# First cross-attention: probabilities transposed in ten packed blocks, V in block form placed by small loads, a third fold on Pool, weights rounded by ScalarE

## The chip, the cores and the metric

The kernel runs on one core of one Trainium2 chip. The metric is the device time of one execution in microseconds (us). TensorE is called PE here, VectorE DVE, ScalarE ACT, GpSimd Pool, and the queue that issues the loads and stores SP. The time before is 2041.48 us, the median of three runs (2040.95, 2041.48 and 2046.44).

## What is computed

Two gated layers on `x` of 4 batches x 1024 tokens x 256, with a context of 4 x 77 x 256. Only the first step of the first layer is touched:

```python
x = x + tanh(g_xattn[0]) * L0_xattn(layernorm(x), ctx, ctx, wq, bq, wk, bk, wv, bv, wo, bo)

# L0_xattn: DIM = 256, 16 heads of 16, SCALE = 16 ** -0.5
qh = heads(q @ wq.T + bq);  kh = heads(k @ wk.T + bk);  vh = heads(v @ wv.T + bv)
attn = softmax(einsum('bhqd,bhkd->bhqk', qh * SCALE, kh))
out = einsum('bhqk,bhkd->bhqd', attn, vh)          # 77 keys
return merge_heads(out) @ wo.T + bo
```

After it come a feed-forward net with ternary weights (1024 hidden), a second cross-attention of 8 heads, and a gated self-attention.

## The kernel before, in words

`gated_layers` runs four stages one after the other: `first_attention` (tag A), `feed_forward` (F), `cross_attention` (C) and a self-attention (E). The change is in `first_attention` alone, which takes the first 255 us or so of the span.

In that stage the 4096 tokens are 16 pairs `n` of 256 tokens, each pair two tiles `T` of 128 (so 32 tiles), four pairs to a batch. `STEPS` runs from -12 to 34, and every engine goes through the same steps in an order written out by hand. In step `T`, with `n, odd = divmod(T, 2)`:

- PE: `scores(T + 2)`; the first two groups of `p_transpose(T)`; `reciprocals(n - 1)` in an odd step or `x_transpose(n + 2)` in an even one; the other two groups of `p_transpose(T)`; `q_proj(n + 2)` (odd); `pv(n - 1, odd)`; `out_proj(n - 2)` (even); and once per batch, in odd steps, `k_proj` and `v_proj`.
- ACT: `prob_out(T, g)` empties PSUM behind the transposes, with `r_evacuate` or `x_evacuate` between the second and third group; then `q_evacuate` (odd), `exp(T + 2)`, `k_evacuate` once per batch, and `layer_norm(n + 3)` (even).
- DVE: `weigh(n - 2)` (even), `row_max(T + 2)`, `shift(T + 2)`, `recip_sum(T + 1)`, `ln_stats`, `v_evacuate` once per batch, `residual(n - 2)` (even), and `mantissas(i)` in the steps of `CHUNK_STEPS`.
- Pool: a third of the Newton step of the next batch's root (`root`), `fold(T + 2)`, `widen(T)`, `add_bias(n)` (odd), and `round_chunk(i)` in the steps of `CHUNK_STEPS`.
- SP: loads and stores in one in-order queue. The chunks are the 22 pieces (128x1024 f32) of the next stage's weights, which are staged in `w_stage` and rounded to fp32r on the way. Chunk `i` is loaded when chunk `i - STAGE` has been rounded (`p_rounded`) and looked at by DVE (`d_bits`).

`p_transpose(T, g)` transposes four heads: per head a 128x77 piece of `prob` is the stationary operand and the identity the moving one, and a 77x128 piece of PSUM comes out. There are two PSUM buffers `ps_t` for the groups, so that group `u` waits for the evacuation of group `u - 2` (`t_out`). A tile has 16 such transposes and four evacuations of 77x512. `pv(n, part)` multiplies the transposed probabilities by V: eight products of 32 columns each, in two rounds over the four column groups of the array; each product is two MATMUL records in the trace. V stands in `vcol`, with 16 of 32 columns filled per head. `fold` halves the 78 columns of `prob` twice on Pool (39, then 20 of 40 padded), and `recip_sum` adds the 20 that are left on DVE.

`scores` has one PSUM buffer: `scores(T + 1)` waits for `shift(T)` (`d_sub`). `layer_norm(n)` waits on ACT for the root of its whole batch (`root_done`); for the first batch DVE works it out in `ln_stats(3)`. `x_transpose(1)` waits for `v_made`, since V's projection of batch 0 stands at step -2 and shares the PSUM buffer `ps_m`.

## Time and profile before

| what | value |
|---|---|
| median of three runs | 2041.48 us |
| the profiled execution | 2043.89 us, its span 2042.2 us |
| PE busy over the span | 1862.7 us (91%) |
| DVE, ACT, Pool busy | 1203.0, 1102.7, 701.8 us |
| stage A, 0 to 256 us | PE 215.11, DVE 189.79, ACT 154.34, Pool 154.35 us busy |

The page gives the busy time of an engine as the sum of its instructions' spans. Matmuls are pipelined: the mean duration of a transpose is 288 ns while the next one starts after about 120 ns, so that what a group of matmuls costs is read from the start of the group to the start of the next group in the timeline, not from a mean duration. Stage F begins when the last pair of stage A has been stored.

### The profile page before, as it was taken

The page shows a single profiled execution, that of the slowest core. Times are in us where ns is not written, and L with a number is a line of the kernel's source. Part 1 is how long each engine was busy: PE and PEld are TensorE (multiplying, and loading weights), DVE is VectorE, ACT ScalarE, POOL GpSimd, SP SyncE. Part 2 cuts the span into 40 slices and gives each one's busy share as a digit, 9 for nine tenths or more (in the row PEclk, how much of TensorE's full clock was granted, in tenths as well). Part 3 has the DMA queues.
Part 4 walks back from the last instruction along what each step waited for, and adds up shares of the span by engine and source line. Part 5 has one row for each costly group of instructions (what it writes and reads, how often), then busy time and mean ns, then how long its engine had stood idle before and what let it go on. Part 6 is the DMA issues. An engine that isn't in the chain of part 4 may idle for free. (4 is left out here: it accounts for less than half of the span.)

```text
span 2042.2 us, 62044 instructions
## 1 busy us (share of the span) xinstructions
PE 1862.7 (91%) x27265; PEld 1520.6 (74%) x27265; DVE 1203.0 (59%) x1687; ACT 1102.7 (54%) x1920; POOL 701.8 (34%) x893
## 2 busy tenths in 40 slices
PE   4999859999999999996799986899999999999986
PEld 3677648888887878875688865778888877887865
DVE  7787532433324333232455535888888888888882
ACT  4677433444434434342455433777777667777761
POOL 3777400100000000100333322556556565655541
PEclk9999979999999999998899997999999999999997
DMA  5222000000000000001101004322332242223110
GB/s 172 81 78 67 27 26 1 21 21 1 21 1 21 21 0 21 0 21 54 64 27 34 23 22 139 87 60 60 101 96 60 60 116 81 65 70 112 55 45 24
DMA packets 135942, 104.95 MB, mean 51 GB/s; under 512 B 9379, under 2 KB 132104, under 8 KB 135688
## 3 DMA queue, kind: packets, MB, share of 16 engines
q1 hardware_dynamic: 135688, 101.19, 16.6%
q8 instruction: 205, 3.36, 0.7%
q14 instruction: 49, 0.40, 0.1%
HBM read 76.00 MB, written 25.17 MB: 50 GB/s over the span
## 5 line engine op out<-in xcount | busy, mean ns | idle before, releaser
L2122 ACT ACTIVATE E_prob<-E_ps_s,E_negmax 128x1024 f32<-128x1024 f32 x256 | 284.7, 1114 | 144.2 <-DVE E_negmax L2436 143.8
L2436 DVE TENSOR_REDUCE E_negmax<-E_ps_s 128x1 f32<-128x1024 f32 x256 | 301.5, 1219 | 88.5 <-PE E_ps_s L1941 88.1
L2443 DVE STREAM_TRANSPOSE E_prob<-E_prob 128x1024 f32<-128x1024 f32 x256 | 304.0, 1226 | 24.0 <-ACT E_prob L2122 11.7
L1960 PEld LDWEIGHTS E_ps_o<-E_prob,E_vrep 32*64 32x64 f32 x15872 | 231.8, 130 | 65.9 <-ACT E_part L2148 56.2
L1960 PE MATMUL E_ps_o<-E_prob,E_vrep 32*64 32x128 f32 x15872 | 263.5, 274 | 13.8 <-issue 4.4
L1544 ACT ACTIVATE F_raw<-F_ps,ffn_scales 128x512 f32<-128x512 f32 x128 | 88.1, 688 | 288.2 <-PE F_ps L1454 288.2
L1454 PE MATMUL F_ps<-F_ha,ffn_w_rounded 128*128 128x512 f32 x1024 | 240.5, 396 | 0.0
L1454 PE MATMUL F_ps<-F_hb,ffn_w_rounded 128*128 128x512 f32 x1024 | 240.2, 395 | 0.0
L1454 PEld LDWEIGHTS F_ps<-F_hb,ffn_w_rounded 128*128 128x128 f32 x1024 | 192.5, 188 | 46.5
L1454 PEld LDWEIGHTS F_ps<-F_ha,ffn_w_rounded 128*128 128x128 f32 x1024 | 191.4, 188 | 47.8 <-issue 1.6
L2338 POOL TENSOR_TENSOR E_part<-E_part 128x512 f32<-128x512 f32 x93 | 119.3, 1283 | 253.8 <-ACT E_part L2148 253.8
L1631 DVE TENSOR_TENSOR F_ha<-F_raw,F_ha 128x512 fp32r<-128x512 f32 x64 | 44.3, 693 | 184.2 <-ACT F_ha L1546 184.2
L1631 DVE TENSOR_TENSOR F_hb<-F_raw,F_hb 128x512 fp32r<-128x512 f32 x64 | 44.4, 693 | 169.1 <-ACT F_hb L1546 169.1
L1454 PE MATMUL F_ps<-F_xt_part,ffn_w_rounded 128*128 128x512 f32 x512 | 125.1, 402 | 11.2 <-DVE F_raw L1621 6.3
L89 POOL TENSOR_TENSOR F_rs<-F_rs 128x4 f32<-128x4 f32 x27 | 5.4, 198 | 358.9 <-DVE F_rs L1592 357.5
L1941 PE MATMUL E_ps_s<-E_k_hi,E_q_hi 64*128 64x512 f32 x512 | 114.7, 443 | 14.1 <-ACT E_prob L2122 12.7
L1454 PEld LDWEIGHTS F_ps<-F_xt_part,ffn_w_rounded 128*128 128x128 f32 x512 | 95.2, 191 | 38.8 <-DVE F_raw L1621 10.6
L1564 POOL TENSOR_TENSOR F_xt_part<-F_xt,F_xt_part 128x1024 fp32r<-128x1024 f32 x9 | 21.6, 2401 | 294.1 <-DMA x<-A_x 149.9
L1941 PE MATMUL E_ps_s<-E_k_hi,E_q_lo 64*128 64x512 f32 x512 | 102.3, 394 | 0.0
L1941 PE MATMUL E_ps_s<-E_k_lo,E_q_hi 64*128 64x512 f32 x512 | 101.2, 390 | 0.0
L472 ACT ACTIVATE A_pt<-A_ps_t 77x512 f32<-77x512 f32 x128 | 69.3, 591 | 28.2 <-PE A_ps_t L359 28.0
L1621 DVE SCALAR_TENSOR_TENSOR F_raw<-F_ps,ffn_scales,F_silu 128x512 f32<-128x512 f32 x64 | 47.5, 750 | 61.8 <-ACT F_silu L1528 61.6
(284 smaller groups left out, 3937.6 us busy)
## 6 DMA issues: line engine op xcount, KB each, us to landing
E_vrep<-E_v_all SPq DMA_DIRECT2D x128, 256.0 KB, 3.1
A_w_stage<-in_L_ffn_h_wT SPq DMA_DIRECT2D x16, 512.0 KB, 4.1
E_v_all<-E_vst SPq DMA_DIRECT2D x32, 256.0 KB, 2.2
F_x<-x SPq DMA_DIRECT2D x9, 512.0 KB, 3.8
A_x<-in_x SPq DMA_DIRECT2D x16, 256.0 KB, 5.6
x<-A_x SPq DMA_DIRECT2D x16, 256.0 KB, 2.2
x<-F_x SPq DMA_DIRECT2D x8, 512.0 KB, 2.9
C_x<-x SPq DMA_DIRECT2D x16, 256.0 KB, 5.5
```

Source lines behind the costliest of these rows:

```text
L472: act.activation(pt[:, n % 2, 4 * g:4 * g + 4, t * TOK:(t + 1) * TOK], ps_t[0:S, g % 2, :].rearrange("s (h q) -> s h q", h=4), ACT.Copy).t ...
L1454: mm = pe.matmul(out, fw.chunk(w, name, k, j * P, (j + 1) * P), a[:, k, :], start=k == 0 and i == 0, stop=k == K - 1 and i == len(parts) - 1)
L1544: act.activation(raw[:, u % 2, :], ps[:, u % 4, :], ACT.Gelu, scale=scale).then_inc(u_raw, 1)
L1564: pool.tensor_tensor(xt_part[1][:, :, :], xt[:, :, :], xt_part[0][:, :, :], ALU.subtract).then_inc(xt_lo, 1)
L1621: dve.scalar_tensor_tensor(out=dst, in0=ps[:, 2 * (j % 2) + 1, :], scalar=scales[:, 1, j:j + 1], in1=silu[:, j % 2, :], op0=ALU.mult, op1= ...
L1631: dve.tensor_tensor(dst, raw[:, u % 2, :], hi, ALU.subtract).then_inc(u_lo, 1)
L1941: mm = pe.matmul(ps_s[:, j, keys], a[rows, c % 2, cols], k[rows, c % 2, keys], start=i == 0, stop=i == 2)
L1960: mm = pe.matmul(low[64 * j:64 * j + 64, g, :], vrep[rows, slot, KB // 4 * (quarter % 2) + k, dh * j:dh * (j + 1)], prob[rows, u % 2, :, j ...
L2122: act.activation(prob[:, s // UT % 2, s % UT, j, :], ps_s[:, j, :], ACT.Exp, bias=negmax[:, at:at + 1], scale=1.0, accum_out=den[:, 2 * c ...
L2338: pool.tensor_tensor(part[:, 0, :], part[:, 0, :], part[:, 1, :], ALU.add).then_inc(part_added, 1)
L2436: dve.tensor_reduce(negmax[:, at:at + 1], ps_s[:, j, :], AX.X, ALU.max, negate=True).then_inc(d_max, 1)
L2443: dve.transpose(at, at).then_inc(d_t, 1)
```

## The change

- `p_transpose` no longer goes head by head. `prob` becomes 1280 columns (`prob_all`: 16 heads of 78 packed, and 32 columns of zeros), and ten blocks of 128 columns are transposed, in groups of 4, 4 and 2. The first group stands ahead of `reciprocals` or `x_transpose`, the other two behind. `prob_out` empties 128x512, 128x512 and 128x256.
- V is laid out for these blocks (`v_blk`, 17 tiles of 128x32): a head's rows stand where the packed probabilities have them. DVE writes V once to `v_sb`, and SP copies it into place by `place_v(b)`, 25 loads per batch of 5 to 77 rows of 64 bytes, since a head's 77 rows can lie across a border of two blocks. `pv` has nine products in part 0 and eight in part 1; the ninth is a third round on one column group.
- Pool folds a third time (20 to 10 columns), and `recip_sum` adds 10.
- `round_chunk` goes from Pool to the end of ACT's step, with `STAGE` 4 in place of 3.
- The first pair gets a root of its own (`root_pair`, from the first two tiles' statistics), and the batch's whole root is then worked out again by DVE for the other pairs.
- V's projection of batch 0 moves from step -2 to -1, and `x_transpose(1)` waits for `q_made` alone.
- The loads of `x` 1 to 3 go behind `wq`. The memsets of `prob_all` and `v_blk` stand on DVE behind the biases, ahead of the first statistics. `place_v(0)` stands in SP's queue behind chunk 4 and ahead of `x` 8 to 11 and chunk 5; `place_v(b + 1)` stands at pair `4 b + 1`.

```diff
-STAGE = 3
+STAGE = 4
...
+    KC = -(-H * S2 // P)
+    GROUPS = [range(k, min(k + 4, KC)) for k in range(0, KC, 4)]
+    NG = len(GROUPS)
+    SEG = HR * S2
+    parts_of = {(g, c): range((g * C + c) * SEG // P, ((g * C + c + 1) * SEG - 1) // P + 1)
+                for g in range(RG) for c in range(C)}
...
         def v_step(b):
 
-            return 2 * PB * b - 3 if b else -2
+            return 2 * PB * b - 3 if b else -1
...
+            def place_v(b):
+
+                sp.wait_ge(v_made, b + 1)
+                if b >= 2:
+                    sp.wait_ge(e_pv, PB * (b - 1))
+                for g, c, j, k, row, n, s0 in v_pieces():
+                    at = (HC * c + HR * g + j) * dh
+                    sp.dma_start(v_blk[row:row + n, b % 2, tile_of[g, c, k], dh * j:dh * (j + 1)],
+                                 v_sb[s0:s0 + n, at:at + dh]).then_inc(s_vblk[b % 2], 16)
...
             load_chunk(STAGE)
+            sp.wait_ge(s_pad, 1)
+            place_v(0)
             for n in range(2 * PB, XR):
                 load_x(n)
...
+                if n % PB == 1 and n // PB + 1 < B:
+                    place_v(n // PB + 1)
                 while at < CHUNKS and CHUNK_STEPS[at - STAGE] <= 2 * n + 2:
                     load_chunk(at)
...
-                elif n % PB == 1:
+                elif n == 2 or n % PB == 1 and n > 1:
                     pe.wait_ge(v_made, n // PB + 1)
...
-                for j in range(4):
-                    mm = pe.transpose(ps_t[0:S, g % 2, j * TOK:(j + 1) * TOK], prob[:, T % PR, 4 * g + j, 0:S],
+                for i, k in enumerate(GROUPS[g]):
+                    mm = pe.transpose(ps_t[:, u % 2, i * TOK:(i + 1) * TOK], prob_all[:, T % PR, k * P:(k + 1) * P],
                                       ident[:, :])
...
-                        h = HC * part + HR * g + j
-                        mm = pe.matmul(ps_o[RT * g:RT * (g + 1), part, :], vcol[:, b % 2, h, :],
-                                       pt[:, n % 2, place(h), :], start=j == 0, stop=j == HR - 1)
+                        ks = parts_of[g, part]
+                        if i < len(ks):
+                            mm = pe.matmul(ps_o[RT * g:RT * (g + 1), part, :], v_blk[:, b % 2, tile_of[g, part, ks[i]], :],
+                                           pt[:, n % 2, ks[i], :], start=i == 0, stop=i == len(ks) - 1)
...
                 if 0 <= T < TILES:
-                    for g in range(G // 2):
-                        p_transpose(T, g)
+                    p_transpose(T, 0)
...
+            def round_chunk(i):
+                act.wait_ge(s_chunk[i % STAGE], 16 * (i // STAGE + 1))
+                act.activation(ffn.w[:, i * WCH:(i + 1) * WCH], w_stage[:, i % STAGE, :], ACT.Copy).then_inc(a_rounded, 1)
...
                 if not odd and 0 <= n + 3 < NP:
                     layer_norm(n + 3)
+                if T in CHUNK_AT:
+                    round_chunk(CHUNK_AT[T])
...
+                own.step(pool.tensor_tensor(quarter[:, :, :], half_sum[:, :, 0:HALF // 2],
+                                            half_sum[:, :, HALF // 2:HALF], ALU.add))
...
+                pool.tensor_tensor(eighth[:, T % 2, :, :], quarter[:, :, 0:HALF // 4],
+                                   quarter[:, :, HALF // 4:HALF // 2], ALU.add).then_inc(p_eighth, 1)
...
+                if n == 0:
+                    own.wait()
+                    for t in range(2):
+                        own.link(dve.bn_aggr(mv0[:, t, :], stats[:, t, :]))
+                    own.wait()
+                    whole_root(mv0, rs0).then_inc(root_pair, 1)
...
-                for j in range(HR):
-                    ins = dve.tensor_tensor(dst[:, :, j, j * dh:(j + 1) * dh], src[:, :, j, :], vb[:, :, j, :], ALU.add)
-                ins.then_inc(v_made, 1)
+                dve.tensor_tensor(v_sb[:, :], ps_m[0:S, 0:HD], vbias[:, :], ALU.add).then_inc(v_made, 1)
...
-            dve.memset(prob[:, :, :, S:S2], 0.0)
-            dve.memset(half_sum[:, :, S2 // 2:HALF], 0.0).then_inc(s_pad, 1)
-            own.link(dve.memset(vcol[:, :, :, :], 0.0))
+            dve.memset(half_sum[:, :, S2 // 2:HALF], 0.0)
...
+            dve.memset(prob_all[:, :, :], 0.0)
+            dve.memset(v_blk[:, :, :, :], 0.0).then_inc(s_pad, 1)
```

`whole_root` is the guess, three Newton steps and the last two products, which before stood in `ln_stats` for the first batch only.

## Rows read from the trace of the kernel before

**Rows 1.** Busy time by engine from step 1 to step 29; start:end, length, engines, clock.
```profile
core 0: us, PE busy (x) PEld busy (x) DVE busy (x) ACT busy (x) POOL busy (x), PEclk, DMA share, GB/s
41.31:231.09 189.78, 177.54 (x1685) 133.06 (x1685) 151.36 (x205) 131.49 (x233) 134.04 (x185) 0.98 0.22 65
```

**Rows 2.** PE's timeline, steps 26 (even) and 27 (odd): start, length, line.
```profile
209.01 0.81 PE L348 MATMUL A_ps_s<-A_kt,A_q 32*128 32x154 f32 x16
209.75 1.10 PE L359 MATMUL A_ps_t<-ident,A_prob 128*77 128x128 f32 x8
210.68 0.60 PE L304 MATMUL A_ps_m<-ident,A_xn 128*128 128x128 f32 x4
211.19 1.11 PE L359 MATMUL A_ps_t<-ident,A_prob 128*77 128x128 f32 x8
212.23 1.07 PE L375 MATMUL A_ps_o<-A_pt,A_vcol 77*32 77x256 f32 x16
213.23 1.99 PE L392 MATMUL A_ps_m<-A_wo,A_o 128*128 128x256 f32 x8
215.15 0.81 PE L348 MATMUL A_ps_s<-A_kt,A_q 32*128 32x154 f32 x16
215.89 1.10 PE L359 MATMUL A_ps_t<-ident,A_prob 128*77 128x128 f32 x8
216.83 0.60 PE L331 MATMUL A_ps_m<-ident,A_r_wide 128*128 128x128 f32 x4
217.33 1.12 PE L359 MATMUL A_ps_t<-ident,A_prob 128*77 128x128 f32 x8
218.29 1.97 PE L316 MATMUL A_ps_m<-A_xt,A_wq 128*128 128x256 f32 x8
...
221.19 0.81 PE L348 MATMUL A_ps_s<-A_kt,A_q 32*128 32x154 f32 x16
```

**Rows 3.** Groups by line and form, 0 to 268 us: busy, mean ns, idle before.
```profile
L472 ACT ACTIVATE A_pt<-A_ps_t 77x512 f32<-77x512 f32 x128 | 69.3, 591 | 28.2 <-PE A_ps_t L359 28.0
L530 POOL TENSOR_TENSOR A_half_sum<-A_prob 128x624 f32<-128x624 f32 x32 | 49.5, 1546 | 71.9 <-ACT A_prob L477 65.4 <-DVE A_rsum L642 3.3 <-issue 2.3
L477 ACT ACTIVATE A_prob<-A_prob 128x1232 f32<-128x1232 f32 x32 | 39.4, 1232 | 13.9 <-DVE A_prob L634 13.9
L534 POOL TENSOR_TENSOR A_quarter<-A_half_sum 128x320 f32<-128x320 f32 x32 | 30.6, 957 | 2.5
L554 POOL CAST ffn_w_rounded<-A_w_stage 128x1024 fp32r<-128x1024 f32 x22 | 23.2, 1056 | 0.3 <-DMA A_w_stage<-in_L_ffn_w_wT 0.3
```

**Rows 4.** ACT's timeline around the start of step 26.
```profile
208.84 1.23 ACT L477 ACTIVATE A_prob<-A_prob 128x1232 f32<-128x1232 f32 x1
210.45 1.08 ACT L472 ACTIVATE A_pt<-A_ps_t 77x512 f32<-77x512 f32 x2 [0.37 <-PE A_ps_t L359]
```

**Rows 5.** Timelines of the start: DVE's memset, ACT's first LayerNorm, DVE's third maximum.
```profile
1.18 0.91 DVE L688 MEMSET A_vcol<- 77x1024 f32 x1
14.34 1.09 ACT L435 ACTIVATE A_xn<-A_x,A_rs 128x256 f32<-128x256 f32 x2 [3.19 <-DVE A_rs L612]
38.27 1.43 DVE L619 TENSOR_REDUCE A_negmax<-A_ps_s 128x16 f32<-128x1232 f32 x1
```

**Rows 6.** Timeline of PE: steps 1 and 3, and the wait of step 11.
```profile
41.31 1.41 PE L348 MATMUL A_ps_s<-A_kt,A_q 32*128 32x154 f32 x16 [5.43 <-DVE A_prob L634]
58.46 1.96 PE L359 MATMUL A_ps_t<-ident,A_prob 128*77 128x128 f32 x8 [3.31 <-ACT A_pt L472]
112.80 1.11 PE L359 MATMUL A_ps_t<-ident,A_prob 128*77 128x128 f32 x8 [1.38 <-ACT A_pt L472]
```

**Rows 7.** SP's queue at the start: issue of a small load, of x, of chunks.
```profile
2.83 0.47 SPq L233 DMA_DIRECT2D A_qbias<-in_L_xattn_bq  x1
16.37 2.13 SPq L206 DMA_DIRECT2D A_x<-in_x  x4
19.67 13.35 SPq L216 DMA_DIRECT2D A_w_stage<-in_L_ffn_h_wT  x3
```

**Rows 8.** DMA issues by line: KB each, median us from issue to landing.
```profile
E_vrep<-E_v_all SPq DMA_DIRECT2D x128, 256.0 KB, 3.1
A_w_stage<-in_L_ffn_h_wT SPq DMA_DIRECT2D x16, 512.0 KB, 4.1
A_x<-in_x SPq DMA_DIRECT2D x16, 256.0 KB, 5.6
```

More of the change, by code:

```diff
@@ L186, in first_attention @@
         x_taken, q_made, k_made, v_made = (sem(n) for n in ("x_taken", "q_made", "k_made", "v_made"))
-        d_sub, a_exp, p_quarter, d_r, p_wide = (sem(n) for n in ("sub", "exp", "quarter_summed", "r", "r_widened"))
+        d_sub, a_exp, p_eighth, d_r, p_wide = (sem(n) for n in ("sub", "exp", "eighth_summed", "r", "r_widened"))
         r_taken = sem("r_taken")
@@ L233, in _ @@
                 sp.dma_start(dst, src).then_inc(s_small, 16)
-            load_x(2)
-            load_x(3)
             load_w(2, wq, wqT)
+            for n in range(1, PB):
+                load_x(n)
             for i, g in enumerate(gates_src):
@@ L410, in _ @@
                 if 0 <= T < TILES:
-                    for g in range(G // 2, G):
+                    for g in range(1, NG):
                         p_transpose(T, g)
@@ L420, in _ @@
                     k_proj((T + 5) // 8)
-                if (T + 3) % 8 == 0 and 1 <= (T + 3) // 8 < B:
-                    v_proj((T + 3) // 8)
+                for b in range(B):
+                    if T == v_step(b):
+                        v_proj(b)
         @block.scalar
@@ L492, in _ @@
                 if 0 <= T < TILES:
-                    for g in range(G // 2):
-                        prob_out(T, g)
+                    prob_out(T, 0)
                 if odd and 0 <= n - 1 < NP:
@@ L499, in _ @@
                 if 0 <= T < TILES:
-                    for g in range(G // 2, G):
+                    for g in range(1, NG):
                         prob_out(T, g)
```

121 lines of the change are left out of this document (67 added, 54 removed).

## The prediction

> **What bounds the kernel now.** I read the table of stretches first, then the timelines of PE, ACT, DVE and SP for stage A, then the groups by line. From step 1 to step 29 PE is busy 177.5 of 189.8 us, DVE 151.4, ACT 131.5, Pool 134.0 [rows 1]. So PE is the bound of the stage once it has started, with a fifth of the time spare on DVE and three tenths on the others. The timeline of steps 26 and 27 shows what this means: each group starts where the last one ends, with no gap [rows 2]. From scores to scores an even step takes 215.15 - 209.01 = 6.14 us and an odd one 221.19 - 215.15 = 6.04, a pair 12.18. Fourteen pairs would be 170.5 us, the projections of K and V some 6; the other 13 us of the 189.8 are waits and stretches of low clock. I look for two things: what leaves PE's pair, and which waits of the other engines come up when the pair is shorter. Ahead of step 1 PE isn't the bound: at 41.31 it had waited 5.43 us for DVE's shift [rows 6].
>
> **PE's pair.** Eight transposes take 0.93 and 1.04 us in the even step and 0.94 and 0.96 in the odd one, 3.87 for the 32 of a pair, 0.12 each [rows 2]. The new ones have 128 columns of weights and not 77. The nearest row is the transposes of x and of the reciprocals, which are 128x128: four take 0.51 and 0.50 us, 0.126 each [rows 2]. Twenty make 2.5 and a tail of 0.1, so 1.27 us leave the pair. V's product gets a third round in part 0. Two rounds take 1.00 us now, and one whole-width product takes 1.92 / 4 = 0.48 (out_proj) [rows 2]. The lone product needs its column group to itself behind two rounds, so I take 0.48; by mere issue (16 records in 1.00 us, two more) it would be 0.12. The net is -0.79 us per pair (bounds -1.4 and, if a transpose cost by its width, +0.5). The first pair lies in the start, so 14.5 pairs: **-11.5 us**.
>
> The Trainium skill ("TensorE: Matmul & The Clock Gate", LDWEIGHTS) speaks against this: a weight load costs by its columns, so that ten loads of 128 columns would cost what sixteen of 77 do. By that rule the transposes gain nothing. The full-width rows above disagree as to the pace, and I weigh it as a rival.
>
> **ACT.** Per tile 4 evacuations at a pitch of 0.49 (two in 1.08 us less the overlap) [rows 4] become two and one of 256 columns. From 1232 columns in 1.23 and 512 in 0.59 us [rows 3] the last is about 0.36, so ACT gains 0.6 us per tile, 19 us in all. The 22 roundings come to it: 1024 columns by the same line, 1.03 us, 23 us. Busy time stays about as it is, and ACT isn't the bound by it. The place matters: in an odd step the rounding stands behind exp(T + 2). Exp ran from 208.84 to 210.07 [rows 4], 1.06 us into step 26, and the first evacuation followed at 210.45. With a rounding between, it starts at S + 2.0 and is done at S + 2.6 (S is the start of the step's scores). PE wants that buffer back for its third group after 0.74 of scores, 4 transposes, 0.5 of x and 4 transposes: S + 2.25. What is queued behind that wait on PE is the last two blocks, V's products and out_proj, so the 0.4 us go onto the path. Fourteen chunks stand in odd steps: 11 at 0.4 and three at 0.8, where k_evacuate stands there too: 6.8, of which the first two are in the start. **+6 us** (bounds 0 and 10). In the three even steps with a chunk ACT has time.
>
> **Pool and DVE.** Pool loses 22 x 1.06 = 23 us and gets 32 folds of 160 columns. From 624 in 1.55 and 320 in 0.96 [rows 3] one is about 0.6 with its wait, 19 us. Its fold chain is 0.6 longer, and done before recip_sum asks for it within 0.5 us. Nothing is due of it until residual, which waits for out_proj anyway: zero, and up to 0.5 per odd step if DVE is late. The cast ahead of the last third of a batch's root leaves, a fold comes: the root is 0.45 us sooner. At step 11 PE waited 1.38 us behind ACT's wait for it [rows 6], and at two other places: **-0.9 us**. DVE gets 0.17 us less per tile. In steps 4 to 7 and 12 to 15, where statistics, chunks, V and the guess meet, DVE's work comes to 25 to 27 us against PE's new 23.5 for four steps (sums of its timeline there); it can lag 1.5 us before scores wait. **+1.5 us** (0 to 5).
>
> **The start.** The memsets now clear 3840 + 1088 columns ahead of the statistics, at 0.91 us per 1024 [rows 5] 4.4 us; three pairs' statistics leave the first root's way, about 2. The first LayerNorm, at 14.34 before [rows 5], comes at about 15.6, and the second, behind a second root of 3.7 us, at 22, 5 us later. The rest is given back in part by x_transpose(1), which no longer waits for V. DVE's third maximum, at 38.27 [rows 5], comes at 40 to 41, and V of batch 0 is made at about 39.
>
> Then SP issues 25 loads. A small load holds the queue 0.47 us [rows 7], so this is 11.8 us (10 to 13). Behind stand x 8 to 11 (2.13 us [rows 7]) and chunk 5: issued at about 53, landed 4.1 to 5.6 us later [rows 8], at 57 to 59. Before, the queue had issued chunks 4 to 6 by 33 [rows 7]. ACT wants chunk 5 at the end of step 1, at about 51, and waits 6.5 us; behind it stands the evacuation of step 2's first group, and so PE's transposes. DVE's mantissas(5) wait for the same load, behind them two passes of 1.43 us [rows 5] until scores(5). That puts q_proj of step 3 at about 65. Before, step 3 lost 3.31 us to the root and went on at 58.46, at the low clock [rows 6], with q_proj at 60.2: this old wait is covered by the new one. **+4.5 us** (1 to 9). V itself lands in time: 51 + 3.1 [rows 8] is where pv(0) falls. The later placements have four steps or more until a chunk behind them is due.
>
> The Trainium skill ("DMA: Bandwidth & Descriptors", Anatomy of one DMA) holds that the fixed cost of a load is nearly all completion latency, setup being small. Alone, it would let the 25 overlap in some 2 us, and the start would cost 1 and not 4.5. The issue rows contradict it for this queue.
>
> **Sum.** -11.5 + 6 - 0.9 + 1.5 + 4.5 = -0.4 us on the profiled 2043.9, so 2043.5. The profiled execution is 2.4 us over the median, which gives 2041.1: **2041 us**.
>
> **Rivals.**
> 1. PE's gain goes through. For it: ACT's busy time doesn't grow, and the two roundings of the start may slip into idle time. If the rounding is hidden (0 for 6) and the start costs 1 to 2, the sum is -11.5 - 0.9 + 1.5 + 1.5 = -9.4: 2032. Against it: ACT's place behind exp leaves no gap in rows 4. Chance 0.30.
> 2. ACT stands before chunk loads. If an issue takes 0.53 us, as in the four loads of x, and the chunk 6.5 us to land behind 1 MB of x, chunk 5 is there at 63 and the start costs 9; the same queue delays the chunks behind place_v(2) and place_v(3), and each rounding then costs its 0.6. -11.5 + 9 + 9 + 3 - 0.9 = +8.6: 2050. It decides from the point where chunk 5 lands 10 us after ACT asks for it. For it: SP's queue is in order; against it: small SBUF loads may issue faster than 0.47. Chance 0.18.
> 3. Transposes cost by the width of the weights (the rule above): 0.12 x 128 / 77 = 0.2 each, no gain, and V's third round: +0.48 per pair. 14.5 x 0.48 + 6 - 0.9 + 1.5 + 4.5 = +18: 2059. The 0.126 of rows 2 speaks against it. Chance 0.04.
>
> The forecast itself has 0.48. The range, 2031 to 2051, takes in most of rivals 1 and 2. 0.3%, about what a measurement of this kernel tells from no change, is 6 us: faster 0.30, same 0.48, slower 0.22.
>
> **What would show it.** In a pair of the late stretch without chunks: scores to scores 11.3 to 11.4 us; groups of four transposes at 0.50 and the last two at 0.25; V's part 0 at 1.45 and part 1 at 1.0. In even steps behind an odd chunk: PE idle 0.4 us before the last group, released by ACT. On SP: 25 issues in 10 to 13 us from about 39. ACT idle some 6 us before the first rounding of the loop, released by a DMA. Clock near 1.00 but for some us at 60. I am wrong on the fast side if the loads issue in under 0.3 us or the roundings leave no wait, on the slow side if DVE or a chunk's load holds PE in every batch.

## The result and the profile after

The changed kernel takes 2052.56 us, the median of 13 runs (2046.88 to 2056.19), where the kernel before took 2041.15 us beside it (13 runs). The ratio is 1.0051, 95% interval 1.0039 to 1.0063: slower by half a per cent, and clear of the spread. The prediction was 2041 us, no change, with a range to 2051; the time lies 1.6 us above that range, and "slower" had a chance of 0.22. The profiled execution of the changed kernel took 2047.0 us, 5.6 under its median; from the last matmul of stage C to the end, which the change doesn't touch, it took 805.4 us, where the profiled executions of all the other kernels took 807.7 to 817.6 (the kernel before 813.9), so I read the stages one by one and not the two spans against each other.

The page of the changed kernel, busy time by engine and the instruction queue (packets, MB, share):

```profile
PE 1847.7 (90%) x27105; PEld 1499.5 (73%) x27105; DVE 1199.1 (59%) x1703; ACT 1101.2 (54%) x1910; POOL 695.2 (34%) x903
...
q8 instruction: 221, 3.62, 0.7%
```

PE is busy 15 us less and the kernel is slower all the same. Three places tell why. First the steady stretch, PE's timeline of steps 26 and 27, which answers to [rows 2]:

```profile
205.92 0.81 PE L384 MATMUL A_ps_s<-A_kt,A_q 32*128 32x154 f32 x16
206.66 0.66 PE L395 MATMUL A_ps_t<-ident,A_prob 128*128 128x128 f32 x4
207.15 0.60 PE L340 MATMUL A_ps_m<-ident,A_xn 128*128 128x128 f32 x4
207.59 0.60 PE L395 MATMUL A_ps_t<-ident,A_prob 128*128 128x128 f32 x4
208.56 0.41 PE L395 MATMUL A_ps_t<-ident,A_prob 128*128 128x128 f32 x2 [0.38 <-ACT A_pt L513]
208.90 1.50 PE L413 MATMUL A_ps_o<-A_pt,A_v_blk 128*32 128x256 f32 x18
210.32 1.99 PE L430 MATMUL A_ps_m<-A_wo,A_o 128*128 128x256 f32 x8
212.25 0.81 PE L384 MATMUL A_ps_s<-A_kt,A_q 32*128 32x154 f32 x16
212.99 0.66 PE L395 MATMUL A_ps_t<-ident,A_prob 128*128 128x128 f32 x4
213.48 0.60 PE L367 MATMUL A_ps_m<-ident,A_r_wide 128*128 128x128 f32 x4
213.91 0.92 PE L395 MATMUL A_ps_t<-ident,A_prob 128*128 128x128 f32 x6
214.91 1.97 PE L352 MATMUL A_ps_m<-A_xt,A_wq 128*128 128x256 f32 x8
216.80 1.07 PE L413 MATMUL A_ps_o<-A_pt,A_v_blk 128*32 128x256 f32 x16
217.81 0.41 PE L384 MATMUL A_ps_s<-A_kt,A_q 32*128 32x154 f32 x4
```

From the start of four packed transposes to the start of the next group is 0.49 us, V's part 0 takes 210.32 - 208.90 = 1.42 and part 1 1.01. The odd step is 217.81 - 212.25 = 5.56 (6.04 before), the even one 6.33 (6.14 before), because it pays 0.38 us of ACT's wait ahead of the last two blocks. ACT's timeline of the same moment, beside [rows 4], has the reason, the rounding between exp and the first evacuation:

```profile
205.75 1.23 ACT L519 ACTIVATE A_prob<-A_prob 128x1232 f32<-128x1232 f32 x1
206.87 1.06 ACT L529 ACTIVATE ffn_w_rounded<-A_w_stage 128x1024 fp32r<-128x1024 f32 x1
207.82 0.59 ACT L513 ACTIVATE A_pt<-A_ps_t 128x512 f32<-128x512 f32 x1
```

Over steps 4 to 29 the table of stretches gives 162.10 us for the changed kernel (77.20 to 239.30); in the kernel before the same steps ran from 64.8 to 231.1, 166.3 us. The stretch is 4.2 us shorter.

```profile
77.20:239.30 162.10, 149.19 (x1405) 104.24 (x1404) 131.85 (x185) 113.39 (x198) 116.88 (x171) 1.00 0.23 71
```

Second, the start: timelines of SP, ACT and PE, beside [rows 7] and [rows 6].

```profile
37.98 19.57 SPq L257 DMA_DIRECT2D A_v_blk<-A_v  x25
57.60 2.04 SPq L229 DMA_DIRECT2D A_x<-in_x  x4
59.74 7.03 SPq L239 DMA_DIRECT2D A_w_stage<-in_L_ffn_h_wT  x5
...
65.15 1.06 ACT L529 ACTIVATE ffn_w_rounded<-A_w_stage 128x1024 fp32r<-128x1024 f32 x1 [16.27 <-DMA A_w_stage<-in_L_ffn_h_wT]
...
66.83 0.66 PE L395 MATMUL A_ps_t<-ident,A_prob 128*128 128x128 f32 x2 [16.75 <-ACT A_pt L513]
67.42 2.78 PE L413 MATMUL A_ps_o<-A_pt,A_v_blk 128*32 128x256 f32 x18
```

The 25 placement loads hold SP for 19.6 us, chunk 5 is issued at 59.7, ACT waits 16.3 us for it and PE 16.8 us for ACT. PE then works on at the slower pace: V's 18 records take 2.78 us instead of 1.50, at a granted clock of 0.50 from 67.42 to 70.20. Step 4's scores come at 77.2, before at 64.8: 12.4 us later. Stage A is left 8.7 us later (first transposes of stage F at 280.48, before at 271.81).

Third, stage F, in which nothing was edited. From its first transposes to the end of its last `F_ps` product, some 9 us before its last matmul, it lasts 679.0 us, before 673.7. All lengths of stage F below are taken so. PE's timeline at two starts of a tile, and the kernel before at the place of the first:

```profile
626.96 3.99 PE L1503 MATMUL F_ps<-F_xt_part,ffn_w_rounded 128*128 128x512 f32 x16 [1.65 <-issue]
797.78 5.54 PE L1503 MATMUL F_ps<-F_xt_part,ffn_w_rounded 128*128 128x512 f32 x16 [1.75 <-issue]
```

```profile
616.43 3.90 PE L1454 MATMUL F_ps<-F_xt_part,ffn_w_rounded 128*128 128x512 f32 x16
```

"Issue" means that PE waited for nothing that the profile shows. The two waits are 3.4 us, and the second group is 1.6 us longer besides (5.54 us for sixteen products instead of 3.90): 5.0 of the 5.3. Both stand where `blocks` jumps back: stage F is a hardware loop (`Fori`) over pairs of tiles, the first pair written out, and the loop's body then runs three times, with two jumps back. The instruction queue shows the same thing. From 640 to 940 us it brings 15 packets of 16 KB in the changed kernel (the view of the DMA queues in this stretch, below) and none in the kernel before.

```profile
q8 instruction: 15, 0.25, 0.3%
```

So the 11.4 us between the medians are, by the profiles, +12.4 in the start, -4.2 in steps 4 to 29, +0.5 in stage A's tail and +5.3 in stage F. That is 14. In the profile of the changed kernel C and E are 11 us shorter than in that of the kernel before, which is why the two spans differ by 3.1 us only; the change doesn't touch these stages, and why they differ was not looked into.

### The profile page after: what moved, and what is told of

Its sections match the earlier page's. It is cut to its first block and busy times, and to the rows that moved or that the text cites. A ratio compares the mean times of both kernels' runs of the same rounds, so it can differ in the third digit from the quotient of the medians.

```text
span 2045.3 us, 61811 instructions
## 1 busy us (share of the span) xinstructions
PE 1847.7 (90%) x27105; PEld 1499.5 (73%) x27105; DVE 1199.1 (59%) x1703; ACT 1101.2 (54%) x1910; POOL 695.2 (34%) x903
## 5 line engine op out<-in xcount | busy, mean ns | idle before, releaser
L2492 DVE STREAM_TRANSPOSE E_prob<-E_prob 128x1024 f32<-128x1024 f32 x256 | 303.9, 1226 | 23.8 <-ACT E_prob L2171 11.5
L1990 PE MATMUL E_ps_s<-E_k_hi,E_q_hi 64*128 64x512 f32 x512 | 114.4, 442 | 13.8 <-ACT E_prob L2171 12.4
L577 POOL TENSOR_TENSOR A_half_sum<-A_prob 128x624 f32<-128x624 f32 x32 | 50.0, 1563 | 86.2 <-ACT A_prob L519 82.8
```

Source lines behind the costliest of these rows:

```text
L577: own.step(pool.tensor_tensor(half_sum[:, :, 0:S2 // 2], prob[:, T % PR, :, 0:S2 // 2], prob[:, T % PR, :, S2 // 2:S2], ALU.add))
L1990: mm = pe.matmul(ps_s[:, j, keys], a[rows, c % 2, cols], k[rows, c % 2, keys], start=i == 0, stop=i == 2)
L2492: dve.transpose(at, at).then_inc(d_t, 1)
```

## The experiments

The question is which part of the change costs what, and where stage F's waits come from. Every kernel but e12's, of which there is one profiled execution, was timed beside the kernel before, whose medians were 2042.9 to 2045.5 us in these groups of runs; so the ratios, and not the medians, are compared from one group to another. A difference of two ratios is uncertain by some 0.0015 to 0.002, 3 to 4 us. Theory A: the loads in SP's queue ahead of chunk 5 cost the start. Theory B: it is the rounding on ACT.

**e1: one placement load instead of 25.** In batch 0 only the first of the loads is issued, 24 are left out.

```diff
-                for g, c, j, k, row, n, s0 in v_pieces():
+                for g, c, j, k, row, n, s0 in list(v_pieces())[:1 if b == 0 else None]:
```

> Of batch 0's 25 small loads of V only the first is issued; the other 24 are left out, so V of batch 0 isn't whole. Theory A (SP's queue: the 25 loads hold it 19.6 us, and chunk 5, x 8 to 11 stand behind them): chunk 5 is issued 18 to 19 us sooner, ACT's wait of 16.3 us before its sixth rounding is gone or under 1 us, scores of step 4 come at 63 to 66 in place of 77.2, and the time is 11 to 13 us under the changed kernel's, so 1 to 3 us under the kernel before. Theory B (the start is long because of the memsets, the second root and the roundings on ACT): step 4 comes at 72 or later and the time falls by under 5 us. Theory C (the 10 us lie in later stages, by their clock): stage A gets shorter but the time stays within 3 us of the changed kernel's.

Measured: 2041.45 us, ratio 0.9995 (0.9981 to 1.0008), step 4's scores at 63.7, stage F entered at 265.5. ACT rounds chunk 5 at once; the timelines of SP and ACT:

```profile
37.34 0.95 SPq L261 DMA_DIRECT2D A_v_blk<-A_v  x1
38.34 2.02 SPq L233 DMA_DIRECT2D A_x<-in_x  x4
40.47 10.07 SPq L243 DMA_DIRECT2D A_w_stage<-in_L_ffn_h_wT  x5
...
49.13 1.06 ACT L533 ACTIVATE ffn_w_rounded<-A_w_stage 128x1024 fp32r<-128x1024 f32 x1
```

The 24 loads are worth 77.2 - 63.7 = 13.5 us, all of the start's loss of 12.4 and a little more; by ratio it is 11 us. Stage F's two waits are still there (3.8 us), so they have nothing to do with the loads.

**e2: the rounding back on Pool.** `round_chunk` as the last thing of Pool's step, as in the kernel before, the rest as changed.

```diff
-                act.activation(ffn.w[:, i * WCH:(i + 1) * WCH], w_stage[:, i % STAGE, :], ACT.Copy).then_inc(a_rounded, 1)
+                pool.tensor_copy(ffn.w[:, i * WCH:(i + 1) * WCH], w_stage[:, i % STAGE, :]).then_inc(a_rounded, 1)
```

> The roundings go back to Pool, with four staging buffers as in the changed kernel; all else as changed. If ACT's place behind exp costs what the idle of 0.4 to 0.9 us per odd chunk shows (14 such waits, 23.0 us with the 16.8 of the start), PE's waits before the last group of transposes go from some 6 us to under 1.5 and steps 4 to 29 take 156 to 158 us in place of 162.1. The root comes 0.5 us later on Pool: up to 1 us back in each of three batches. Pool instead of ACT then waits for chunk 5, and PE may still stand 10 us or more there, as folds are late. Net 3 to 6 us under the changed kernel. Rival: the roundings were hidden and Pool's longer chain takes it back: within 2 us.

Measured: 2061.9 us, ratio 1.0094 (1.0078 to 1.0110). That is 9 us worse than the changed kernel, not better. The profiles show 3.7 us of it in the stages A and F (stage F entered at 283.5, 3.0 us later, with waits of 4.0 us); the rest lies behind them and is not explained. ACT is free in the start, but PE now meets the placement loads themselves and then DVE, as its timeline shows:

```profile
60.03 2.78 PE L413 MATMUL A_ps_o<-A_pt,A_v_blk 128*32 128x256 f32 x18 [5.45 <-DMA A_v_blk<-A_v]
70.67 1.41 PE L384 MATMUL A_ps_s<-A_kt,A_q 32*128 32x154 f32 x16 [7.85 <-DVE A_prob L689]
```

**e3: V of batch 0 earlier.** V's projection stands directly behind K's, DVE writes it out at step -12, and SP places ten pieces, issues chunk 4, and places the other fifteen, from 17 us on.

```diff
-            return 2 * PB * b - 3 if b else -1
+            return 2 * PB * b - 3 if b else -5
...
-            load_chunk(STAGE)
             sp.wait_ge(s_pad, 1)
-            place_v(0)
+            place_v(0, 0, 10)
+            load_chunk(STAGE)
+            place_v(0, 10)
```

> V of batch 0 is projected right behind K, while PE has nothing to do (7.4 to 17.2 us in the changed kernel), and evacuated by DVE behind the first root; SP issues 10 of its loads, chunk 4, and the other 15 in the time in which it waits for nothing else. Nothing is left out. Theory A: the loads run from about 17 to 37 us, chunk 5 is issued at about 39 and landed at 44, ahead of ACT's need at 49; ACT's wait is gone; step 4 at 62 to 66; the time 12 to 15 us under the changed kernel's, 2 to 4 under the kernel before. Theory B: the start stays 8 us or more longer than before. By theory A it beats the kernel before by 0.1 to 0.2%.

Measured: 2040.12 us, ratio 0.9989 (0.9974 to 1.0003), step 4's scores at 65.8, stage F entered at 268.2. SP is done with the placement by 37.3 us and chunk 5 is there in time. 77.2 - 65.8 = 11.4 us of the loss are back, with all the work in place: theory A holds, and the loads cost by where they stand.

**e4: e3 with the rounding on Pool.**

> Both edits: V of batch 0 early, and the roundings on Pool. If the two losses are separate they add: 12 to 15 us for the start and 3 to 6 for the waits behind ACT, so 16 to 20 under the changed kernel, 2033 to 2036 us, 0.3 to 0.45% under the kernel before. A pair without waits takes 11.5 us as in the changed kernel. If DVE or Pool becomes the bound once ACT's waits are gone, the second gain is under 2 us.

Measured: 2051.18 us, ratio 1.0044 (1.0027 to 1.0061), 11 us over e3. The waits of 0.38 us are gone as theory B has it (step 10 takes 5.9 instead of 6.3 us), but steps 11 and 19 take 11.9 and 11.3 us where e3 needs 7.7, and stage F is entered 7.6 us later than in e3. Pool's and PE's timelines of step 19:

```profile
165.61 1.28 POOL L599 TENSOR_TENSOR A_x<-A_x,A_obias 128x512 f32<-128x512 f32 x1
166.83 1.04 POOL L604 CAST ffn_w_rounded<-A_w_stage 128x1024 fp32r<-128x1024 f32 x1
167.83 0.21 POOL L89 TENSOR_TENSOR A_rs<-A_rs 128x8 f32<-128x8 f32 x1
```

```profile
171.32 0.41 PE L401 MATMUL A_ps_t<-ident,A_prob 128*128 128x128 f32 x2 [2.98 <-ACT A_pt L519]
171.81 3.31 PE L358 MATMUL A_ps_m<-A_xt,A_wq 128*128 128x256 f32 x8
```

The cast stands ahead of the root's last third, ACT waits for that root, PE for ACT, and after 2.98 us of idling PE's next eight products take 3.31 us instead of 1.97. With the third fold on Pool there is no room for the cast as well; the rounding on ACT, which I had priced as the change's cost, is its better half.

**e5: the odd step's rounding ahead of the evacuation of q**, so that it no longer stands between exp and the first evacuation of the next step (e3 otherwise).

```diff
+                if odd and 0 < T and T in CHUNK_AT:
+                    round_chunk(CHUNK_AT[T])
                 if odd and 0 <= n + 2 < NP:
                     q_evacuate(n + 2)
```

> As e3 (V early), and in odd steps ACT rounds its chunk ahead of q_evacuate, where it stood idle 1.3 us per odd step behind PE's q_proj, in place of behind exp. Theory: the waits of PE for ACT behind odd chunks (0.38 or 0.8 us at the third group of the next even step, 14 of them in steps 1 to 27) go, since exp is followed at once by the evacuation of the first group; nothing is added, because q_proj ends after the rounding does. Pairs with an odd chunk take 11.5 us in place of 11.9, steps 4 to 29 some 157 us in place of 162.2, the time 4 to 6 us under e3's. Rival: q_evacuate is delayed by the rounding and scores wait for it (0.3 us or more per odd chunk); then no gain.

Measured: 2049.38 us, ratio 1.0034 (1.0020 to 1.0049), 9 us over e3. Earlier in the step the chunk has not landed in some batches. ACT's and SP's timelines:

```profile
99.04 1.06 ACT L535 ACTIVATE ffn_w_rounded<-A_w_stage 128x1024 fp32r<-128x1024 f32 x1 [2.50 <-DMA A_w_stage<-in_L_ffn_h_wT]
```

```profile
75.34 19.85 SPq L257 DMA_DIRECT2D A_v_blk<-A_v  x25
95.31 0.90 SPq L239 DMA_DIRECT2D A_w_stage<-in_L_ffn_h_wT  x2
```

Each later batch's placement holds the queue 19.9 us too, and PE waits 11.1 us for q in six places (e3: 4.4 in three). What this costs is less sure: its waits for ACT's evacuations fall from 9.8 to 6.0 us, and in the profiled execution, the fastest of the eight (2042.59 us), the stages A and F are only 2.9 us longer than in e3. The other 6 us of the ratio are not shown by a trace. The prediction's "the later placements have four steps until a chunk is due" is true only as long as the rounding stays late.

**e6: e5 with the memset of the probabilities cut to the pads**, 0.24 us of DVE where 3.26 stood.

```diff
-            dve.memset(prob_all[:, :, :], 0.0)
+            dve.memset(prob[:, :, :, S:S2], 0.0)
+            dve.memset(prob_all[:, :, H * S2:KC * P], 0.0)
```

> As e5, and DVE clears only the padding columns of the probabilities (48 and 96 columns) in place of all 3840. Theory: the first root is 3.0 us sooner, LayerNorm(0) at 13 in place of 16, and the start up to the second root with it. If DVE's chain carries the start, step 4 comes 2 to 3 us sooner than e5's, and the time is 2 to 3 us under e5's. If the wait of step 3 for the root of the second batch hides it, less than 1 us. Over both, 2031 to 2035 us, under the kernel before by 0.3 to 0.5%.

Measured: 2044.44 us, ratio 1.0000 (0.9987 to 1.0013). Meant as the best version, it is not: the waits of e5 are in it. The ratio is 0.0034 under e5's, but stage F is entered at 272.6 against 269.0, so the trace doesn't show the gain in stage A, and I don't put it to the memset.

**e7: e3 without the third fold.** DVE sums the 20 quarters again.

```diff
-                own.step(pool.tensor_tensor(quarter[:, :, :], half_sum[:, :, 0:HALF // 2],
-                                            half_sum[:, :, HALF // 2:HALF], ALU.add))
-                pool.tensor_tensor(eighth[:, T % 2, :, :], quarter[:, :, 0:HALF // 4],
-                                   quarter[:, :, HALF // 4:HALF // 2], ALU.add).then_inc(p_eighth, 1)
+                pool.tensor_tensor(quarter[:, T % 2, :, :], half_sum[:, :, 0:HALF // 2],
+                                   half_sum[:, :, HALF // 2:HALF], ALU.add).then_inc(p_eighth, 1)
```

> As e3, without the third fold: Pool folds twice and DVE adds 20 columns, as before the change. Pool has 0.6 us less per tile, DVE 0.17 us more. The wait of PE for the batch's root (0.9 and 0.8 us at steps 11 and 19 and the long one at step 3) gets shorter by up to 1.2 us each, as two folds stand ahead of the last third; DVE's waits for the fold (5.5 us in all) go. The pairs stay at 11.5 to 11.9. Net 1 to 3 us under e3. If the third fold helps DVE where the bound is, the time is 1 to 3 us over.

Measured: 2035.29 us, ratio 0.9965 (0.9952 to 0.9978): the first that beats the kernel before. Step 4's scores come at 61.1 (65.8 in e3), steps 11 and 19 take 7.0 us (7.7), stage F is entered at 262.6 (268.2).

**e8: e7 with the rounding on Pool.**

> As e7, and the roundings on Pool: what remains of the change is the packing, V in blocks, and V early. e4 lost 11 us against e3 by Pool's rounding together with the third fold, 2.7 to 4.6 us at each batch's root and the low clock behind it. If Pool's sum of work ahead of the root is the cause, then without the third fold the waits fall back to 1.4 us at steps 11 and 19 as in the kernel before, and the time is 8 us or more under e4's, about 2 to 4 us under e3's, since ACT's waits are gone as well. If Pool's rounding alone is the cause, it stays within 3 us of e4's.

Measured: 2044.38 us, ratio 0.9999 (0.9986 to 1.0011). By ratio it is 7 us over e7 and 9 under e4. So, by these ratios, the rounding on Pool costs 7 us without the fold and 11 with it, and the fold 5 us without the rounding and 9 with it: each delays the root, and together they cost most. The difference between the two pairs, 4 us, is no larger than their error, but the traces show it at steps 11 and 19: the rounding on Pool makes these two 7.8 us longer with the fold (e4 against e3) and 3.4 us without (e8 against e7). Of e8's 7 us nearly all arises ahead of step 4, whose scores come at 68.4 (e7: 61.1); a batch of eight later steps costs 0.6 us more, since the root takes what the waits for ACT give back.

**e10: the changed kernel without the third fold**, the placement left where the change has it.

> The changed kernel with the third fold alone taken out: VectorE sums quarters again, the rest stays, the 25 placements ahead of the chunk loads too. Theory F (the fold lengthens Pool's chain ahead of the root once a batch, 0.6 to 0.7 us at the root steps and 2 us at step 3): stage A ends 5 us earlier than in the changed kernel (280.5, so about 275.5), steps 11 and 19 take 7.0 us instead of 7.6, and the median is 4 to 5 us lower, about 2048. Rival G (in the changed kernel the start is set by ScalarE's wait for a chunk, so the fold is hidden there, and only the steady root steps gain): 1 to 2 us, about 2051.

Measured: 2052.91 us, ratio 1.0047 (1.0030 to 1.0064). By ratio that is 0.8 us under the changed kernel, and less than the error. Theory F misses; rival G's mechanism holds, and its 1 to 2 us can't be told from what was measured. Steps 11 and 19 do take 7.0 us instead of 7.6, but step 4's scores come 1.5 us later (78.7), since V is made 0.5 us later and ACT's rounding of chunk 5 starts at 66.1 instead of 65.1, and stage F is entered at 280.4 as in the changed kernel (280.5). The fold's 5 us in e3 lay mostly in the start, and there the wait for chunk 5 covers it.

**e11: e7 with the small memset of e6.**

> The fastest kernel so far (V of batch 0 projected behind K, ten placements, a chunk, fifteen placements, two folds) and in it the memset of the probabilities reduced to the pads, 0.4 us instead of 3.3 us of VectorE at 7 us. Theory H (VectorE is on the path of the start, since its layer norms follow the memset): step 4's scores come 1 to 3 us earlier than 61.1, and the median is 2034, 1 to 2 us under that kernel's 2035.3. Rival I (the wait for x and for Q sets the start, VectorE has slack): step 4 stays within 0.5 us of 61.1 and the median within 1 us of 2035.3.

Measured: 2035.99 us, ratio 0.9967 (0.9953 to 0.9981). Step 4's scores come 0.8 us earlier (60.3), between the two expectations, and stage F is entered 1.3 us later (263.9), as step 19 takes 7.7 instead of 7.0 us. I count the memset as no gain.

**e12: what the issue of one placement costs SP, in four forms.** Batches 1 to 3 place other data than V, so this kernel computes something else; it has one profiled execution.

```diff
+                    if b % 2:
+                        row, n, s0 = 0, 64, 0
+                    if b >= 2:
+                        sp.dma_start(v_blk[row:row + n, b % 2, tile_of[g, c, k], dh * j:dh * (j + 1)],
+                                     wvT[s0:s0 + n, 0:dh]).then_inc(s_vblk[b % 2], 16)
+                        continue
```

> One look at what the issue of one placement load costs SyncE, in four forms, one for each batch; batches 1 to 3 place other data, so that the output is not the reference's. Batch 0: as in the change (source v in SBUF, 4 to 77 rows, odd first rows). Batch 1: the same source, 64 rows each, first row 0. Batch 2: the rows of batch 0, the source a weight matrix in HBM. Batch 3: HBM and 64 rows each. Theory R (the issue costs by source: from SBUF more): batches 0 and 1 at 0.74 to 0.78 us a load, batches 2 and 3 at 0.45 to 0.55, as the two bias loads of the kernel before had 0.47. Rival S (by the count and place of the rows): batches 0 and 2 alike at 0.75, with a spread of 0.59 to 0.95, and batches 1 and 3 alike, without spread. Rival T (by how many loads stand in a row, whatever their form): all four at 0.74 to 0.78.

Measured, SP's timeline, batches 0 to 3 in order:

```profile
37.80 19.60 SPq L263 DMA_DIRECT2D A_v_blk<-A_v  x25
90.58 16.64 SPq L263 DMA_DIRECT2D A_v_blk<-A_v  x25
142.13 10.45 SPq L259 DMA_DIRECT2D A_v_blk<-in_L_xattn_wvT  x25
193.68 16.57 SPq L259 DMA_DIRECT2D A_v_blk<-in_L_xattn_wvT  x25
```

A load takes 0.78, 0.67, 0.42 and 0.66 us. None of the three theories fits. The loads of 64 rows cost the same from SBUF and from HBM, which speaks against R; the change's uneven pieces cost 0.78 from SBUF and 0.42 from HBM, which speaks against S; and T is out. What is shown is that the form of a load moves its issue by a factor of almost two on this queue, and that the HBM bias load from which I took 0.47 us [rows 7] stands for 0.42 and not for 0.78. The rule stays open. The changed kernel's trace narrows it: the same piece takes the same time in all four batches, mostly to 0.01 us, and the number of its rows hardly matters: the piece of 5 rows takes 0.71 us and those of 77 rows mostly 0.76 to 0.84.

**e9, e13 to e16: the waits of stage F.** Neither the loads (e1, 3.8 us), nor the rounding (e2, 4.0), nor the fold (e7, 3.9, and e10, 3.7) removes them. Theory L: it matters where in PE's stream of instructions the loop begins; in some places its body stays resident, in others it is fetched again in every iteration. I put one-column matmuls that nobody reads ahead of the loop: in e9 80 of them far ahead, behind K's first projection; in e13, e14 and e15 20, 40 and 60 just ahead of stage F in e7's kernel; in e16 40 in the kernel before.

```diff
+            for _ in range(40):
+                pe.matmul(ps_x[:, 0, 0:1], ident[:, :], ident[:, 0:1], start=True, stop=True)
             pe.wait_ge(ln, 1)
             x_transpose(0)
```

> The changed kernel with eighty one-column matmuls added behind K's projection of batch 0, where TensorE stands idle anyway; they write a bank that is overwritten later and nothing waits for them. They bring the count of TensorE's instructions before stage F back to about what the kernel before has. Theory P (the two waits of TensorE in stage F that end in 'issue', 3.7 us together in the changed kernels and none in the kernel before, hang on how many instructions TensorE has behind it when it gets there): the waits move or go, stage F lasts 674 to 676 us instead of 678 to 679, and the median is 2 to 4 us under the changed kernel's, about 2049. Rival Q (they hang on something else, such as a transfer of that moment): both waits stay at their places with 3.7 us, and the median stays within 1.5 us of the changed kernel's 2052.6.

> The fastest kernel so far (e7) with 20 one-column matmuls ahead of stage F's first transposes, in 17 us in which TensorE waits for VectorE; nothing reads them. Theory L (whether the loop's body stays in the engine's instruction memory hangs on where it begins in the stream): for at least one of the numbers 20, 40 and 60 both issue waits at the loop's jumps back (3.9 us in e7) are gone, the fetches from 640 us on fall to about 2, and stage F lasts 674 instead of 678 us; that kernel's median is 3 to 4 us under e7's 2035.3. Rival M (the waits come from another thing that the change brought): all three numbers leave both waits at 1.6 to 2.1 us. Under both, the matmuls may take 0 to 2.5 us off stage F's first tile, since TensorE enters it at a higher granted clock.

> As e13_loop_pad20, with 40 one-column matmuls, 17 us at the 0.21 us that each of their two passes took in e9. Theory L: the waits are gone for at least one of the three numbers; rival M: they are there in all three, 3.6 to 3.9 us together.

> As e13_loop_pad20, with 60 one-column matmuls. At 0.43 us each, as in e9, they would take 26 us and reach 9 us over the idle time, at the 0.12 us a pass of a weight load at full clock 14 us and nothing. Theory L: the waits are gone for at least one of the three numbers; rival M: they are there in all three.

> The kernel before with 40 one-column matmuls at the same place. Theory L: its loop too can be moved to a place where its body is fetched in every iteration; then two issue waits of 1.6 to 2.1 us stand in stage F, which lasts 677 to 679 us instead of 674, and the median is 3 to 5 us over the kernel before's. A third to a half of the places would do that, if one number has to answer for all, so that no wait speaks against the theory only weakly. Rival M: no wait appears, and the median stays within 1.5 us of the kernel before's 2043.

Measured (stage F from its first transposes to the end of its last `F_ps` product; packets of the instruction queue from 640 to 940 us):

| kernel | added | issue waits in F | packets | stage F | ratio to before, 95% |
|---|---|---|---|---|---|
| before | 0 | none | 0 | 673.7 us | 1 |
| changed | 0 | 3.4 us, 2 | 15 | 679.0 us | 1.0051 (1.0039 to 1.0063) |
| e7 | 0 | 3.9 us, 2 | 14 | 678.0 us | 0.9965 (0.9952 to 0.9978) |
| e9 | 80, changed kernel | 3.6 us, 2 | 17 | 677.0 us | 1.0167 (1.0149 to 1.0185) |
| e13 | 20, e7's | 6.8 us, 4 | 13 | 682.5 us | 0.9976 (0.9959 to 0.9992) |
| e14 | 40, e7's | none | 0 | 673.6 us | 0.9971 (0.9961 to 0.9981) |
| e15 | 60, e7's | 4.0 us, 2 | 15 | 677.6 us | 1.0046 (1.0030 to 1.0061) |
| e16 | 40, before | 3.6 us, 2 | 15 | 677.6 us | 1.0024 (1.0014 to 1.0035) |

The views of the waits of e13 and e16, and PE's timeline of e14 at the jump back, where no wait stands:

```profile
PE F_ps L1506 <- issue: 6.8, 4, 1.9
```

```profile
PE F_ps L1454 <- issue: 3.6, 2, 2.0
```

```profile
607.61 7.78 PE L1548 MATMUL F_ps_y<-ffn_w_rounded,F_ha 128*128 128x256 f32 x64
615.24 3.90 PE L1506 MATMUL F_ps<-F_xt_part,ffn_w_rounded 128*128 128x512 f32 x16
```

Theory L holds in both directions: 40 added matmuls take the waits and the fetches out of e7's kernel and bring them into the kernel before. Theory P, that with as many instructions ahead as in the kernel before the waits go, is out: e9's 80 bring the number back to nearly that, and its waits stay. The traces hold, of PE and PEld together, 3997 instructions ahead of stage F in e14 (as in e17 and e18 below) and 4189 in the kernel before, which have no wait, and 3837, 3917, 4077, 4157 and 4349 in the changed kernel (as in e7), e13, e15, e9 and e16, which have them. Places with and without waits alternate, so no single threshold of this number would explain them. In e9 the added work took 34.2 us and stood ahead of Q, which I had not reckoned with: step 4's scores come at 100.3, 23.1 us later. The 60 of e15 and the 40 of e14 reached 15 and 8 us over the idle time (stage F's first transposes at 277.5 and 270.7 instead of 262.6), and e16's 40 reached 9 us over it; these three medians therefore carry the added work too, and the verdict rests on the waits and the packets. In e13 each of the two jumps back has two waits, 3.6 us together at the first and 3.2 at the second.

**e17 and e18: the same number, in idle places.** e17 is the changed kernel with 20 behind K's first projection and 20 ahead of stage F; e18 is e7 with 10 behind V's first projection, 10 behind stage A's last output projection and 20 ahead of stage F.

> The changed kernel with 40 one-column matmuls more, as in e14, but 20 of them behind K's projection of batch 0 (TensorE idle for 9.8 us) and 20 ahead of stage F (idle for 17 us). Theory L (the loop's place decides, and 40 is a good number): no issue wait in stage F, 674 us for it from its first transposes without the added matmuls, and a median 3 to 5 us under the changed kernel's 2052.6, so about 2048.5, still 5 to 6 us over the kernel before. Rival M (4 us of the loss lie elsewhere behind stage A): stage F is cured, and the median stays above 2050.5.

> The fastest kernel (e7: V of batch 0 projected behind K, two folds) with the 40 one-column matmuls spread over idle places: 10 behind V's projection, 10 behind the last output projection of stage A, 20 ahead of stage F. Theory L: no issue wait in stage F, the fetches gone, stage F's start within 1 us of e7's 262.6, and a median of 2031 to 2032.5 against e7's 2035.3, a ratio of about 0.9945 to the kernel before. Rival M: the median stays within 1.5 us of 2035.3.

Measured: e17 2048.89 us, ratio 1.0016 (1.0002 to 1.0029), and e18 2035.63 us, ratio 0.9950 (0.9935 to 0.9965). Both are without waits and packets in stage F (673.7 and 673.4 us, as the kernel before). By ratio e17 is 0.0035 under the changed kernel, about 7 us, with the intervals allowing 3.5 to 11, so the 5.3 us from the loop fit and a little more is not told apart. e18 against e7 is 0.0015, 3 us, within the error; that its loop gains 4.6 us is read from the profiles (673.4 against 678.0 us). It has the lowest ratio of the study, 0.5% under the kernel before.

Not tested singly are the root of the first pair, the fourth staging buffer, the moved loads of `x`, and the packing with V in blocks. The nearest to the packing alone is e8 (ratio 0.9999), which still has 3.8 us of the waits of stage F.

## Why the prediction failed, step by step

The step that failed is the term of the start, +4.5 us: it was reckoned with 0.47 us for the issue of a placement load, and an issue took 0.78. A second term, for stage F, was missing from the sum.

- **PE's pair: right.** Without the ACT wait the pair is (6.33 - 0.38) + 5.56 = 11.51 us, said 11.3 to 11.4, so 0.67 us left the pair and not 0.79; transposes 0.49 to 0.50 for four, V's part 0 1.42 (said 1.45). Full-width transposes cost what 77-wide ones do, 0.12 us each, so rival 3 (the rule of the Trainium skill, "TensorE: Matmul & The Clock Gate", LDWEIGHTS) did not come about.
- **ACT's roundings: right in mechanism**, nine waits of 0.37 to 0.38 us at the place named and one of 0.81 in steps 4 to 29, 4.2 us where about 6 was said; the three steps with `k_evacuate` cost 0.6 and not 0.8 (0.37 and 0.19). Where the prediction weighed them as the cost of the change, e2, e4 and e8 show that leaving them on Pool costs 7 to 11 us by ratio, 3.7 to 9.3 in the stages A and F of the profiles.
- **Sum of the steady terms: right, with errors that cancel**, -4.9 said, -4.2 measured over steps 4 to 29. The pair's gain there is 8.7 us (0.67 for thirteen pairs; 11.5 was said, 0.79 for 14.5), the roundings cost less than said, and in place of the waits of 0.16 to 0.35 us that PE had for ACT before. DVE costs 2.3 us (said 1.5): part 0 of V's product waits 0.88 us for it in each of steps 6, 14 and 22, 2.6 us where 0.3 stood. Steps 11 and 19 are 1.0 us shorter each, about 0.5 more than an odd step such as 27, which bears out the -0.9 for the root.
- **The third fold: wrong.** It was set at zero because nothing on Pool was due. The root is on Pool in the same steps, and ACT waits for the root: e3 against e7 is 0.0024, 5 us. In the changed kernel it hides under the start's wait (e10) but for 0.6 us in each of steps 11 and 19, so it is not what put the forecast off.
- **The start: the mis-sized term.** The order of events came as written: first LayerNorm at 16.0 us (said 15.6), second at 22.2 (22), third maximum at 39.0 (40 to 41), V made at 38 (39), and then 25 loads, ACT's wait for chunk 5 and PE's for ACT. The term that failed is the 0.47 us of an issue. It took 0.78, so 19.6 us and not 11.8; chunk 5 was issued at 59.7 and not 53, and rounded at 65.1; ACT's wait was 16.3 and not 6.5 us, and the start cost 12.4 and not 4.5 us. Of the 9.8 us more of ACT's wait, 7.8 are the issues; ACT asked 2.1 us sooner, at 48.9, and the landing took 5.4 us instead of the 4.5 that the prediction's 6.5 us imply, while the issues began 1 us sooner. That the loads are the cause is shown by e1; the split is arithmetic on the trace, and 4.5 + 7.8 = 12.3 is the start as measured. Rival 2 had this mechanism with 0.53 us an issue and 9 us for the start, and its 2050 is nearest to the result; but that is partly luck, since ACT waited for no chunk between 77 and 239 us, where it put 3 us, the roundings cost about half of the 9 us it gave them, and stage F was not in it. Both ends of my range for an issue lay below the measured one, since I took it from a load of another form. The Trainium skill's rule that was cited for the opposite ("DMA: Bandwidth & Descriptors", Anatomy of one DMA) is written for loads that GpSimd issues, while these are issued by SP. Here the 25 issues take 19.6 us one behind the other, and only the 5.4 us of chunk 5's landing come to them.
- **Behind stage A: left out.** The sum had no term for stages that the change doesn't touch, and stage F gave +5.3 us, for the place of its loop in PE's stream. With the start's 12.4 in the sum it comes to 2041.1 + 7.9 + 5.3 = 2054, against 2052.6 measured. Without stage F's 5.3 us, and all else as it was, the time would have lain within the range, near its slow end.

## What to carry to other kernels

Price the issue of a small load by a load of the same form, source and row pattern, and multiply it by the number of loads before asking when they land: what stands behind them in the queue pays. When work moves between engines, look for the chain with the longest dependence on the receiving engine (here the root on Pool), not for its busy share. A kernel with a hardware loop should be looked at for waits released by "issue" at the jump back and for packets on the instruction queue inside the loop; here some instructions more or less ahead of it were worth 3.6 to 5.3 us, some 0.2%, with no change to the work.

## What the runs showed of the hardware that I had not expected

- A loop whose body has to be fetched again costs 1.6 to 2.1 us at each jump back here (in e13 3.6 and 3.2), and the same body at another place in the stream costs nothing. An iteration takes 797.78 - 626.96 = 171 us, so the 15 packets of 300 us are 8 or 9 of 16 KB for each. Which places are good was not worked out; 0, 20, 60 were bad and 40 good for e7's kernel, and 0 good and 40 bad for the kernel before.
- A one-column f32 matmul is not small. Its two records took 0.214 us each in the start and 0.217 ahead of stage F, where the granted clock was 0.50 (the lower of the two levels), and 0.114 us each behind stage A's last projection at clock 1.00, about what a transpose with 128 moving columns takes (0.12). Each record goes with a load of 128 columns of weights; that this sets the pace was not tested. For the start the view prints a clock of 1.00 too (e18, 12.65 to 16.90), beside the pace of the lower level. The trace holds no record of the clock before 22.3 us, and the view prints 1.00 where there is none, so which level was granted in the start is not known. PE's timeline of e18:

```profile
12.65 4.26 PE L332 MATMUL A_ps_o<-ident 128*128 128x1 f32 x20
245.99 2.29 PE L469 MATMUL A_ps_s<-ident 128*128 128x1 f32 x20
251.87 8.69 PE L1517 MATMUL F_ps_x<-ident 128*128 128x1 f32 x40 [3.59 <-PEq L38]
```

- The issue of a small load holds SP for 0.42 to 0.78 us by its form (e12), with single ones at up to 1.6 us. In the changed kernel a given piece takes the same time in every batch, mostly to 0.01 us.
